# Scatter groups of three for the last 30 tiles, the last pair's nodes in its later tile, and early gathers paced by transposes

## What is computed

```python
h = jnp.maximum(_layernorm(x), 0.0)                      # eps 1e-5, no gain or bias
x_ij = jnp.concatenate([h[src], h[dst]], axis=1)         # (12500, 1024)
m_ij = jax.nn.relu(x_ij @ W.T + b)                       # (12500, 512)
out = x + jax.ops.segment_sum(m_ij, src, num_segments=50000)
```

## Time and profile before

| | |
|---|---|
| median of three runs | 740.54 us |
| the profiled execution | 739.76 us |
| its span, first to last instruction | 737.9 us |
| PE busy | 703.2 us, 95% of the span |
| DVE, ACT, POOL busy | 593.8, 470.1, 365.5 us |
| granted TensorE clock, mean | 0.986 |
| DMA moved | 182.36 MB, 247 GB/s mean |

### The profile page before, as it was taken

The page is one execution under the profiler, slowest core; times in us unless marked ns, Lnnn a source line. Parts: engine busy times, 40 slices in busy tenths (PEclk is TensorE's granted clock), DMA queues, the critical chain, the costliest instruction groups (busy, mean ns, idle before and its releaser), DMA issues.

```text
span 737.9 us, 12931 instructions
## 1 busy us (share of the span) xinstructions
PE 703.2 (95%) x3448; PEld 584.3 (79%) x3448; DVE 593.8 (80%) x2001; ACT 470.1 (64%) x892; POOL 365.5 (50%) x305
## 2 busy tenths in 40 slices
PE   3599999999999999999999999999999999999992
PEld 2478888888888888888888888888888888888881
DVE  6488888888888888888888888888888789777861
ACT  5377576576666757757667666675765766766640
POOL 7433233232232322323137777767777777777644
PEclk9799999999999999999999999999999999999997
DMA  7999999999999999999968787777878787878765
GB/s 250 398 380 378 365 377 351 348 365 356 362 362 369 364 368 359 356 376 353 362 146 136 148 135 150 131 144 130 145 139 143 141 142 143 139 148 133 134 87 71
DMA packets 35713, 182.36 MB, mean 247 GB/s; under 512 B 7018, under 2 KB 7342, under 8 KB 33048
## 3 DMA queue, kind: packets, MB, share of 16 engines
q0 software_dynamic: 29792, 77.00, 50.2%
q1 hardware_dynamic: 5504, 104.87, 37.5%
q10 hardware_dynamic: 392, 0.20, 0.1%
HBM read 156.44 MB, written 128.09 MB: 386 GB/s over the span
## 4 chain that ended last, share of the span: by engine, by line
PE 83%; DMA 4%; POOL 4%; issue 3%; ACT 3%; another core or an unknown queue 1%; DVE 0%; ACTq 0%; POOLq 0%
PE z_ps L639 22%; PE z_ps L637 22%; PE z_ps L638 21%; PE ht_ps L621 10%; DMA out<-ring,add_i 4%; PE agg_ps L646 4%; PE agg_ps L647 4%; POOL out L229 3%; POOL xg L209 1%; ACT w_hi L473 1%; ACT ht_hi L480 0%; ACTq L465 0%; ACT xg L496 0%; ACT xg L487 0%
## 5 line engine op out<-in xcount | busy, mean ns | idle before, releaser
L209 POOL DMA_INDIRECT xg<-x,node_i x196 | 204.8, 1045 | 264.4 <-PE ht_ps L621 218.3
L637 PE MATMUL z_ps<-w_hi,ht_hi 128*128 128x512 f32 x784 | 316.3, 403 | 8.4 <-DVE ht_lo L299 8.4
L639 PE MATMUL z_ps<-w_hi,ht_lo 128*128 128x512 f32 x784 | 309.4, 395 | 0.0
L638 PE MATMUL z_ps<-w_lo,ht_hi 128*128 128x512 f32 x784 | 307.6, 392 | 0.0
L480 ACT CAST ht_hi<-ht_ps 128x512 fp32r<-128x512 f32 x194 | 104.4, 590 | 215.6 <-PE ht_ps L621 184.9
L229 POOL DMA_INDIRECT out<-ring,add_i x98 | 158.3, 1615 | 101.3 <-DMA out<-ring,add_i 60.7
L637 PEld LDWEIGHTS z_ps<-w_hi,ht_hi 128*128 128x128 f32 x784 | 148.5, 189 | 36.9 <-DVE ht_lo L299 8.6
L639 PEld LDWEIGHTS z_ps<-w_hi,ht_lo 128*128 128x128 f32 x784 | 148.1, 189 | 32.5
L638 PEld LDWEIGHTS z_ps<-w_lo,ht_hi 128*128 128x128 f32 x784 | 148.4, 189 | 30.0
L496 ACT ACTIVATE xg<-xg,rstd 128x512 f32<-128x512 f32 x194 | 130.1, 725 | 1.9 <-issue 1.5
L299 DVE TENSOR_TENSOR ht_lo<-ht_ps,ht_hi 128x512 fp32r<-128x512 f32 x194 | 124.8, 685 | 8.0 <-ACT ht_hi L480 7.7
(11 more groups left out here) (64 smaller groups left out, 360.1 us busy)
## 6 DMA issues: line engine op xcount, KB each, us to landing
out<-x SPq DMA_DIRECT2D x125, 800.0 KB
xg<-x,node_i POOLq DMA_INDIRECT x196, 3.5
ring<-w_chunks SPq DMA_DIRECT2D x4, 512.0 KB, 4.7
out<-ring,add_i POOLq DMA_INDIRECT x98
row_lanes<-src_rows ACTq DMA_DIRECT2D x49, 4.0 KB
bias_bc<-bias SPq DMA_DIRECT2D x1, 256.0 KB
node_i<-node_cols SPq DMA_DIRECT2D x1, 98.0 KB, 1.9
```

What stands on the lines that cost most here:

```text
L209: nc.gpsimd.indirect_dma_start(out=xg[:, b, s, :], out_offset=None, in_=x, in_offset=bass.IndirectOffsetOnAxis(ap=node_i[:, column:column ...
L637: nc.tensor.matmul(z_ps[b][:, :], hi, w_hi[:, c, :], start=(c == 0), stop=False)
L638: nc.tensor.matmul(z_ps[b][:, :], hi, w_lo[:, c, :], start=False, stop=False)
L639: last = nc.tensor.matmul(z_ps[b][:, :], lo, w_hi[:, c, :], start=False, stop=(c == K - 1))
```

## The change

- TRIPLES goes from 6 to 10, so FIRST3 from 78 to 66: 33 pairs, 10 triples, and the last pair.
- In the last pair the later tile (97) takes the nodes of both: tile 96 has position 1 and tile 97 position 0. Tile 96's sum is complete before tile 97 is multiplied; two matmuls follow the last products where there were four. POOL waits for `add_ready` of each of the two tiles apart.
- RAMP = 4: the gathers of tiles 4 to 11 wait for transposes (tile 4 for tile 0, tiles 5 and 6 for tile 1, 7 and 8 for tile 2, 9 and 10 for tile 3, 11 for tile 4); before, those of tiles 4 to 7 waited for none, and tile t of 8 to 11 for tile t-8. From tile 12 on nothing changes.

The diff, cut to its core:

```diff
-    TRIPLES = 6
+    TRIPLES = 10
     FIRST3 = TILES - 2 - 3 * TRIPLES
+    RAMP = 4
...
-            if not isinstance(t, int) or t < FIRST3 or t >= TILES - 2:
+            if not isinstance(t, int) or t < FIRST3:
                 return b, t - b, 2
+            if t >= TILES - 2:
+                return 1 - b, t - b, 2
...
-                if t >= XS:
-                    pool.wait_ge(transposed, SIDES * (t - XS + 1))
+                if t >= RAMP:
+                    pool.wait_ge(transposed, SIDES * (max(t - XS, (t - RAMP + 1) // 2) + 1))
...
-                pool.wait_ge(add_ready, first + size)
+                if group < len(GROUPS) - 1:
+                    pool.wait_ge(add_ready, first + size)
                 for t in range(first, first + size):
+                    if group == len(GROUPS) - 1:
+                        pool.wait_ge(add_ready, t + 1)
...
+                elif isinstance(t, int) and t == TILES - 2:
+                    dve.wait_ge(row_arrived[m // 2], 2 * (t - m) + 16)
+                    for half in range(2):
+                        nc.vector.stream_shuffle(src_row[:, half * P:(half + 1) * P],
+                                                 row_lanes[:, m // 2, (1 - half) * P:(2 - half) * P], [0] * LANES
+                                                 ).then_inc(row_spread, 1)
+                    dve.wait_ge(row_spread, t + 2)
...
-            nc.vector.tensor_copy(ring[:, (TILES - 1) % RING, :], agg_ps[1][:, :]).then_inc(last_filled, 1)
+            nc.vector.tensor_copy(ring[:, (TILES - 1) % RING, :], agg_ps[0][:, :]).then_inc(last_filled, 1)
...
-            for s in range(RING + 3 + XS * rounds, TILES + 1):
+            for s in range(RING + 3 + XS * rounds, TILES):
                 step(s, s % XS, again=True)
             act.wait_ge(scattered, 16 * (TILES - RING))
-            store_sum(TILES - 2, 0, True)
+            store_sum(TILES - 2, 1, True)
+            step(TILES, TILES % XS, again=True)
...
+            def first_of_last_pair(t):
 
                 pe.wait_ge(same_ready, t + 1)
                 pe.wait_ge(ring_filled, t)
                 pe.wait_ge(mlo_ready, t + 1)
...
+                sum_of(1, ((2, 1),))
+                nc.tensor.matmul(agg_ps[0][:, :], same[:, 1, :], m_hi[:, 1, :], start=True, stop=False)
+                nc.tensor.matmul(agg_ps[0][:, :], same[:, 1, :], m_lo[:, 1, :], start=False, stop=False)
+
+            def second_of_last_pair(t):
+
+                pe.wait_ge(same_ready, t + 1)
+                pe.wait_ge(mhi_ready, t + 1)
+                nc.tensor.matmul(agg_ps[0][:, :], same[:, 0, :], m_hi[:, 0, :], start=False, stop=False)
+                pe.wait_ge(mlo_ready, t + 1)
+                nc.tensor.matmul(agg_ps[0][:, :], same[:, 0, :], m_lo[:, 0, :], start=False, stop=True
                                  ).then_inc(agg_done, 1)
```

More of the change, by code:

```diff
@@ L671, in last_sum_of_triple @@
                 sum_of(0, ((5, 2),))
-            def first_half_of_last_pair(t):
+            def first_of_last_pair(t):
                 pe.wait_ge(same_ready, t + 1)
@@ L677, in first_half_of_last_pair @@
                 pe.wait_ge(mlo_ready, t + 1)
[L678 to L689, removed]
-                nc.tensor.matmul(agg_ps[1][:, :], same[:, 2, :], m_lo[:, 1, :], start=False, stop=True
+                sum_of(1, ((2, 1),))
[7 more added lines that the diff above has]
+                nc.tensor.matmul(agg_ps[0][:, :], same[:, 0, :], m_lo[:, 0, :], start=False, stop=True
                                  ).then_inc(agg_done, 1)
@@ L728, in _ @@
             products(TILES - 1, 1, (0,))
-            first_half_of_last_pair(TILES - 2)
+            first_of_last_pair(TILES - 2)
             products(TILES - 1, 1, (1,))
-            second_half_of_last_pair(TILES - 2)
+            second_of_last_pair(TILES - 1)
 def kernel(x, src, dst, L0_gnn_W, L0_gnn_b):
```

## The result

The changed kernel takes 749.13 us (median of 20 runs, 747.04 to 754.69) where the kernel before takes 740.59 beside it (20 runs): a ratio of 1.012, 95% interval 1.0109 to 1.0132. It is slower by 1.2%. That is inside the 2% called no change, but above the forecast of 743.6 and just outside its range, which ended at 748.5. The profiled execution has a span of 746.7 us where 737.9 was.

What follows compares the result with a forecast made beforehand. The chain of adds ends the kernel, PE close behind; PE's lateness of 6.0 us (2.7 matmuls, 3.3 waiting) holds back the chain's gain, moving the end +3.1 us: 743.6 us against the median, range 734.5 to 748.5.

Steps and rivals of the forecast that it cites:

- The bound, and the sizes of the chain: At the end, POOL's chain of adds bounds the kernel, PE close behind; triples 9.86 us apart, pairs 7.5.
- the chain's -5.6: Tiles 66 to 77: four triples for six pairs make the chain of adds 5.6 us shorter.
- PE's 2.7 us: On PE, 12 more matmuls for the added triples make everything behind tile 78 come 2.7 us later.
- The gathers: Late gathers of tiles 94 to 97 make PE wait 3.3 us; queued DVE work charged nothing; bounds 0 to about 4 more.
- rival C: Slower by more: PE's waits of 2.2 and 1.1 us cost it the clock, 747.6 us; chance 0.15.
- The tail: Last groups: tile 93's sum at 722.2, last group 9.4 us later at 731.6, span end at 741.0.
- The last pair: At the last sums and adds, both orders of the pair give the same end within 0.6 us; taken as 0.
- The pacing: Early gathers: pacing may remove PE's 8.4 us idle at the start; end unmoved, 0, bounds -1 to +1.
- A: The chain's gain comes through: gathers arrive in time, the end moves by -5.6 us to 735.0; chance 0.17.
- B: No net effect: gathers just suffice, PE late by its 2.7 us alone, 740.3 us; chance 0.20.

Runs made afterwards that it cites:

- three_sides: The changed kernel with three gather instructions behind each of the first six triples: 744.88 us, ratio 0.9927 to the kernel before.
- dve_order: The changed kernel with DVE's bias, comparison, low parts and message low part ahead of its statistics from step 85 on: 744.93 us, ratio 1.0063.
- six_triples: The changed kernel with six triples again, keeping the paced gathers and the new last pair: 739.24 us, ratio 0.9985.
- three_sides_old_pair: As three_sides, but with the last pair of the kernel before: 743.64 us, ratio 0.9944.
- pacing_only: The kernel before with the paced early gathers as the only edit: 747.82 us, ratio 1.0026.
- after again: The changed kernel, unaltered, run once more in the third set: 758.72 us, ratio 1.0141 to the kernel before.
- t10_only: The kernel before with ten triples as the only edit, without pacing or new last pair: 747.96 us, ratio 1.0105.

## Why the prediction was wrong

**The bound, and the sizes of the chain.** Right. The first add at 376.40, triples 9.7 us apart, gathers within 1.4 us of their forecast, the adds of tile 93 released by ACT's store. Most of the chain's -5.6 is there to be had, as three_sides shows (4.8 by its timeline); in the changed kernel it is spent on waiting.

**PE's 2.7 us.** Not seen apart. In the changed kernel PE is ahead at tile 91 (660.45, where before it was at 663.8), since it has neither the stall nor the low clock behind it. That lead makes its waits longer and changes nothing in where they end.

**The gathers.** Here the forecast fails, in one sentence of it: "the low parts of tile 93 are still done some 5 us after the landing, when PE is at the transposes of tile 94, so I charge nothing". It names the message among what waits behind the late landing, but prices it at nothing, and looks at tile 94's step alone, which has no sums ahead of its transposes. Landing to transposes was taken as 5.1 us at every tile. For tile 94 that holds: its landing is at 684.51, its transposes were forecast for 690.6 and came at 689.85. In the two steps with a triple's sums it is twice as long: 10.7 us for tile 92 (664.87 to 675.56), where only PE's lead is used up, and for tile 95. For tile 95 the landing was at 694.35 and 5.1 would give 699.5; the transposes came 10.7 us after it, at 705.01, where the forecast had 700.4. That is 4.6 us, and it stays to tile 97: 718.23 against 713.6. Its parts: the sums could have begun at 700.4 - 2.3 = 698.1 and began at 701.05, 2.95 us; then 1.65 for the clock. I had looked at what is queued behind the wait in DVE, but not at who stands in PE's queue between that work and the transposes. The ten matmuls of the sums stand there in one step of three. dve_order took only this away and put tile 97 at 714.2, 4.0 us earlier, though with a loss of clock of its own. The clock is the second thing that the sum had at nothing: it stood only in the bounds of this term and in rival C.

**The tail.** Working right, its input wrong. Store to adds, and 9.4 us from group to group (9.55 measured) carry the 4.6 us on; POOL issues the adds 1.4 us after the store begins, where I had 0.6. Together 741.0 + 4.6 + 0.8 + 0.2 = 746.6; the span is 746.7.

**The last pair.** Nothing, as forecast: six_triples at 0.9985 and three_sides_old_pair against three_sides. One figure of that step is misread: half of the time from the first of the four matmuls (724.49) to the store (725.89) is 0.7 us, not 0.35. The result doesn't hang on it.

**The pacing.** Nothing at the end, as forecast. But the reason I could not give is now half there. PE's stall at 22 us is in four of the six unpaced profiles and in none of the twelve paced ones, so pacing does remove it, in every profile here. It cost a wait at the sums of the start (about 1.6 us at 39 us), and the end of the changed kernel hangs on gathers, so 8 us of lead were waited away. With the adds in place it is worth nothing (pacing_only 1.0026, slower if anything); without them 7.6 us in one set and nothing in another, where the unpaced kernel had no stall. What holds ACT's release in an unpaced execution stays open.

**The rivals.** A fell: the gathers are late. B fell with it. C was the mechanism, with both of its parts, the clock and "a DVE queue held up by late statistics"; but its 747.6 had put a number to the clock alone, and at tile 95 the other part is the larger. The kernel before shows how little slack there is in such a step, DVE's low part of tile 92's message and the first of the sums that use it:

```profile
690.32 0.68 DVE L350 SCALAR_TENSOR_TENSOR m_lo<-zb,m_hi 128x512 fp32r<-128x512 f32 x1
```
```profile
692.11 0.39 PE L646 MATMUL agg_ps<-m_hi,same 128*128 128x512 f32 x1
```

It is 692.11 - 691.00 = 1.1 us, and the forecast itself had the gather of tile 95 some 14 us later than before. By these two rows the queue had a price. From the start of the statistics (684.73) to the end of the message's low part it is 6.3 us, and the ten matmuls take 2.3: with a landing at 689.8 + 5.3 = 695.1 that puts the transposes of tile 95 at 703.7 instead of 700.4. Those 3.3 us make 746.9 of the forecast's 743.6, and 750.9 of C's 747.6, above the end of the range. The measured 749.13 lies between the two.

## What to carry to other kernels

Where an in-order engine waits at the head of its step for a late transfer, price everything that stands behind that wait, and then what stands ahead of the consumer on the *other* engines' queues; a circle through two queues can double the way from a landing to its use. When a chain of dependent DMAs shares its queue with loads, count both per group: fewer, larger groups must carry their share of the loads, and no more than the landing time hides. And start from the step that is heaviest for the consumer, since a mean step has slack where that one has none.

## What was not expected of the hardware

- PE's clock fell to 0.50 and 0.56 behind single waits of 3.94 and 4.43 us in a stretch otherwise without gaps, and ten matmuls took 4.4 and 4.0 us in place of 2.3. Shorter waits did it too: 3.18 us in dve_order (0.50) and 2.49 us in six_triples (0.61). But behind one of 2.98 us in after again, at 672.90, it stayed at 1.00 (672.9 to 679.0), so the length of the wait alone doesn't tell. Behind a wait of 1.35 us (at 660.45) there is no such loss: from the second on, the matmuls of the products that follow start 0.23 us apart, at 661.80, 662.03 and 662.25.
- A stall of 8.2 to 8.4 us at about 22 us, that comes with eight gathers issued at once in the start, in 4 of 6 such profiles, and in none of 12 with paced gathers. By the mean granted clock of the unpaced kernel without adds it was in all four runs of one set (0.992 to 0.995) and in none of another (1.00).
- A gather of two times 128 rows can take very long beside the copy: in t10_only the rows of tile 48, asked for at 303.73, are used at 355.82, and DVE waited 5.38 us for them.
- The kernel before differs by 1.2% between sets of runs (740.6 to 749.1 us), and the copy's end by some 7 us. Two of the sets that differ (740.6 and 747.7 us) bear the same chip number; the cause stays open.
